# Mixing's output computed inside the scan's block, on the 32-column blocks of the diagonal

## The reference, cut to what matters

```python
def step(s, inp):
    q_, w_, k_, v_, a_, b_ = inp
    sa = jnp.einsum('bhij,bhj->bhi', s, a_)
    s = s * w_[:, :, None, :] + sa[..., None] * b_[:, :, None, :] + v_[..., None] * k_[:, :, None, :]
    return (s, jnp.einsum('bhij,bhj->bhi', s, q_))
...
mu = yg.mean(-1, keepdims=True)                       # over the 8 channels of a head
var = ((yg - mu) ** 2).mean(-1, keepdims=True)
y = ((yg - mu) / jnp.sqrt(var + EPS)).reshape(Bx, Tx, C) * ln_w + ln_b
rk = (r.reshape(Bx, Tx, H, HS) * k.reshape(Bx, Tx, H, HS) * time_faaaa.reshape(H, HS)).sum(-1, keepdims=True)
y = y + (rk * v.reshape(Bx, Tx, H, HS)).reshape(Bx, Tx, C)
return y * g @ Wo.T
...
x = _layernorm(x + mixing(x)); x = _layernorm(x + six_layers(x))
```

## Time and profile before

| what | us |
|---|---|
| median of 3 runs shown | 2058.27 (2057.75 to 2066.3) |
| the profiled execution's own time | 2050.26 |
| its span in the trace | 2048.5 |
| scan's last DVE instruction ends | 255.2 |
| first DVE instruction of the output's block | 260.86 |
| first product of the chain on PE | 283.11 |
| last start of the chain written by DVE | 321.87 |
| last part of the starts ends on PE | 336.9 |
| last copy of the output's block on ACT ends | 376.47 |
| first DVE instruction of the six layers' block | 379.30 |

### The profile page before, as it was taken

One profiled execution on the slowest core, in us unless ns is written; L12 is line 12 of the kernel. 1 busy time (PEld: TensorE's weight loads), 2 busy tenths in 40 slices (PEclk: granted clock), 3 DMA queues, 4 the chain that ended last, 5 costly groups with the idle time before them and its releaser, 6 DMA issues. The chain is left out here.

```text
span 2048.5 us, 74276 instructions
## 1 busy us (share of the span) xinstructions
PE 1858.8 (91%) x31234; PEld 1300.1 (63%) x31234; DVE 1515.7 (74%) x2858; ACT 1249.4 (61%) x2435; POOL 1225.9 (60%) x771
## 2 busy tenths in 40 slices
PE   7487778489999999999999999999999999999984
PEld 2254467156677776767666777677676767776762
DVE  6699854477778787777777787778777777878753
ACT  6422111366767767676767677676767676776761
POOL 3466610186767666766766676667666666766630
PEclk9799975699999999999999999999999999999996
DMA  4333000322222224232242222422324222222220
GB/s 98 53 40 43 1 21 0 142 68 64 71 62 70 65 64 121 63 75 63 71 116 69 63 68 65 118 66 64 74 64 122 64 68 63 68 65 63 70 59 21
DMA packets 89900, 137.41 MB, mean 67 GB/s; under 512 B 27296, under 2 KB 32864, under 8 KB 88544
## 3 DMA queue, kind: packets, MB, share of 16 engines
q1 hardware_dynamic: 89568, 132.67, 26.9%
HBM read 29.80 MB, written 2.10 MB: 16 GB/s over the span
## 5 line engine op out<-in xcount | busy, mean ns | idle before, releaser
L1086 POOL TENSOR_TENSOR qk<-qk,rnorm 128x1024 f32<-128x1024 f32 x192 | 361.1, 1902 | 369.6 <-ACT rnorm L1311 369.6
L1080 POOL TENSOR_TENSOR qk<-qk,turnedhalf 128x1024 f32<-128x1024 f32 x192 | 454.5, 2367 | 138.2 <-DVE turnedhalf L1437 138.2
L1433 DVE TENSOR_TENSOR qk<-bank,gains 128x512 f32<-128x512 f32 x384 | 262.1, 683 | 235.7 <-ACT squares L1301 224.5
L1137 PE MATMUL bank<-wqkv,x 128*128 128x512 f32 x768 | 378.6, 596 | 22.3 <-DMA qk_gain<-in_qk_gain 20.4
L1301 ACT ACTIVATE squares<-bank 128x512 f32<-128x512 f32 x384 | 232.8, 606 | 168.9 <-PE bank L1137 167.1
L1437 DVE TENSOR_TENSOR turnedhalf<-bank,gains 128x256 f32<-128x256 f32 x768 | 285.2, 412 | 0.0
L1348 ACT ACTIVATE o_T<-bank 128x512 f32<-128x512 f32 x192 | 104.2, 598 | 230.8 <-PE bank L1201 230.6
L1443 DVE TENSOR_REDUCE rnorm<-squares 128x16 f32<-128x1024 f32 x192 | 230.7, 1201 | 3.0 <-issue 0.2
L1201 PEld LDWEIGHTS bank<-p_T,v_win 64*64 64x64 f32 x12288 | 189.5, 135 | 59.4 <-issue 57.6
L1150 PEld LDWEIGHTS bank<-st_ident,qk 128*128 128x128 f32 x1536 | 178.0, 142 | 56.9 <-issue 50.7
L1201 PE MATMUL bank<-p_T,v_win 64*64 64x32 f32 x12288 | 201.3, 220 | 7.5 <-issue 7.4
(11 more groups left out here) (196 smaller groups left out, 3064.8 us busy)
## 6 DMA issues: line engine op xcount, KB each, us to landing
v_win<-v_tok SPq DMA_DIRECT2D x1536, 64.0 KB
wqkv<-in_wqkv SPq DMA_DIRECT2D x6, 1536.0 KB
v_rep_sb<-v_by_step SPq DMA_DIRECT2D x32, 128.0 KB
v_rep<-v_by_step SPq DMA_DIRECT2D x32, 128.0 KB
wo<-in_wo SPq DMA_DIRECT2D x6, 512.0 KB
w<-in_w SPq DMA_DIRECT2D x6, 341.0 KB
w<-in_w SPq DMA_DIRECT2D x6, 192.0 KB
xT_sb<-in_xT SPq DMA_DIRECT2D x1, 1024.0 KB, 4.7
```

The costliest lines, as they stand in the source:

```text
L1080: nc.gpsimd.tensor_tensor(out=qk[n % 2][:, half], in0=qk[n % 2][:, half], in1=turnedhalf[:, half], op=ALU.add).then_inc(rot_added.sem, 1)
L1086: nc.gpsimd.tensor_tensor(out=by_head(qk[u][:, half]), in0=by_head(qk[u][:, half]), in1=rnorm[u][:, AH * i:AH * (i + 1)].unsqueeze(2).to_b ...
L1137: nc.tensor.matmul(QK_BANKS[i][:, :], shifted_tokens(x, n, P), layer_cols(wqkv, n, 3 * INNER, 512 * i, 512), start=True, stop=True).then_i ...
L1433: nc.vector.tensor_tensor(by_head(qk[u][:, cols]), src, cos.to_broadcast([P, 8, DH]), ALU.mult).then_inc(rotated.sem, 1)
```

## The change

`build_scan` and `build_mix_output` become one function, `build_steps`, with one block. Its main parts:

- **End of the scan.** In the last step DVE makes the final G ahead of problem 0's last update: `end_g` into a PSUM bank, then spreads the first 8 chunks of each sequence (`spread_g_first`) and turns them with its own 32x32 transpose (`make_prop`). ACT copies G to SBUF (`copy_g`), POOL spreads the other 48 chunks (`spread_g`, 6 instructions), and DVE turns them at n = 4, 10 and 18 of the chain.
- **The diagonal.** A 128x128 block-diagonal matrix of 8x8 blocks has non-zeros only in four 32x32 blocks. `spread` and `prop` keep these alone: 32 columns for each chunk in place of 128. Each product of the chain and of `part_of_starts` is then four matmuls of 32 rows by 32 columns (`quads`), on the diagonal of the array.
- **Bonus.** rk on POOL in four pieces during the scan (`r_times_k`, at l = 2, 10, 18, 26), summed on PE at l = 25 to 28 (`product_rk`) with a matrix that has the vector in it, copied by ACT, multiplied with v by POOL during the chain.
- **During the chain.** The scan's last y product (8 matmuls, `last_y`) is issued two matmuls at a time behind chain(1) to chain(4). The parts of starts stand behind chain(9) to (12), (17) to (20), (25) to (28), (29) and (30), four products each; the last eight follow the chain. Groups 0 and 2 (the first half of each sequence) are centred, squared and scaled during the chain; `centre` is one matmul with (identity - ones/8) in place of a sum and a subtraction.
- **Behind the chain.** Groups 1 and 3 follow. For each group: `unit_y` (one operation, with ln_w in it), `gate_y` (two), the projection into one bank (4 matmuls), one addition of x for 512 columns, statistics, its own 1/sqrt as exp(-0.5 ln) on ACT, the norm, the turn, and two copies of 512 columns on ACT in place of eight of 128. The block's second ACT table load goes.

```diff
-def build_scan(nc, t, banks, v_dram, v_rep, state):
+def build_steps(nc, a, t, banks, v_dram, v_rep, state, y, zy, x_mid, x):
...
+            def make_prop(e, s):
+                cs = chunks(s, EIGHT * e, EIGHT * (e + 1))
+                if e:
+                    dve.wait_ge(g_spread.sem, B * (e - 1) + s + 1)
...
+                nc.vector.transpose(prop[:, cs, :].rearrange("p c m -> p (c m)"), spread[:, cs, :].rearrange("p c m -> p (c m)")).then_inc(prop_made.sem, 1)
...
             for l in range(CHUNK):
...
                 if l + 1 < CHUNK:
                     times_a(1, l + 1)
+                else:
+                    end_g()
+                    for s in range(B):
+                        spread_g_first(s)
+                    for s in range(B):
+                        make_prop(0, s)
                 renew0(l)
...
+            end_h()
...
+            for n in range(START):
+                next_start(n)
+                if n in (4, 10, 18):
+                    make_prop({4: 1, 10: 2, 18: 3}[n], 0)
+                    make_prop({4: 1, 10: 2, 18: 3}[n], 1)
+                if n == 20:
+                    whole_y(0)
+                if n == 21:
+                    whole_y(2)
+                if n == 27:
+                    unit_y(0)
+                if n == 28:
+                    unit_y(2)
+            whole_y(1)
+            whole_y(3)
+            gate_y(0)
+            gate_y(2)
+            add_x(0)
+            unit_y(1)
+            gate_y(1)
+            unit_y(3)
+            add_x(2)
+            gate_y(3)
+            norm_x(0)
+            add_x(1)
+            norm_x(2)
+            add_x(3)
+            norm_x(1)
+            norm_x(3)
...
+                if l % STEPS == 2:
+                    r_times_k(l // STEPS)
...
+            def quads(out, left, right, cols):
+
+                for q in range(P // QUAD):
+                    part = slice(QUAD * q, QUAD * (q + 1))
+                    mm = nc.tensor.matmul(out[part, cols], left[part], right[part], start=True, stop=True, skip_group_check=True)
+                return mm
...
+                    quads(CHAIN_BANKS[s], prop[:, c, :], start[:, c, :], slice(0, HS)).then_inc(chain_product.sem, 1)
...
+            for n in range(START):
+                chain(n)
+                if 1 <= n <= 4:
+                    last_y(2 * n - 2)
+                    last_y(2 * n - 1)
+                if 9 <= n <= 12:
+                    part_of_starts(2 * (n - 9), 2 * (n - 8))
...
+                if n == 22:
+                    centre(0)
+                if n == 23:
+                    centre(2)
+                if n == 24:
+                    variance(0)
+                if n == 25:
+                    variance(2)
...
+            part_of_starts(28, 32)
+            centre(1)
+            centre(3)
+            project(0)
+            variance(1)
+            project(2)
+            variance(3)
+            project(1)
+            turn_x(0)
+            project(3)
+            turn_x(2)
+            turn_x(1)
+            turn_x(3)
```

More of the change, by code:

```diff
@@ L459, in _ @@
                 in_step(l, stages)
+                if l == CHUNK - 1:
+                    copy_g()
                 copy_state(l)
@@ L575, in _ @@
                 in_step(l, stages)
-            dve.wait_ge(s_copied.sem, CHUNK)
-            last = decay[:, N:N + CHUNKS].unsqueeze(1).to_broadcast([P, HS, CHUNKS])
-            for p in range(2):
-                dve.wait_ge(s_new[p].sem, CHUNK)
-                nc.vector.tensor_tensor(rows(state[:, p, :]), rows(S_BANKS[p][:, :]), last, ALU.mult).then_inc(ended.sem, 1)
+            end_h()
+            for s in range(B):
+                nc.vector.memset(start[:, SEQ_CHUNKS * s, :], 0.0).then_inc(start_set.sem, 1)
@@ new lines, in _, with next_start @@
+            nc.vector.memset(x[64:P, :, 0:1], 0.0).then_inc(x_edged.sem, 1)
+            H = state[:, 0, :].rearrange("p (r c) -> p c r", c=CHUNKS)
+            def next_start(n):
+                for s in range(B):
+                    c = SEQ_CHUNKS * s + n
+                    dve.wait_ge(chain_product.sem, B * n + s + 1)
+                    if n == 0:
+                        dve.wait_ge(ended.sem, 1)
+                    nc.vector.tensor_tensor(start[:, c + 1, :], CHAIN_BANKS[s][:, 0:HS], H[:, c, :], ALU.add).then_inc(started.sem, 1)
@@ new lines, in norm_x @@
+            def norm_x(j):
+                dve.wait_ge(ln_made.sem, place(j) + 1)
+                for n in range(PER * j, PER * (j + 1)):
+                    nc.vector.tensor_scalar(x_mid[:, n, :], x_tok[:, n, :], ln_mv[:, n, 0:1], ln_mv[:, n, 1:2],
+                                            ALU.subtract, ALU.mult).then_inc(normed.sem, 1)
+            for n in range(START):
[11 more added lines that the diff above has]
+                    unit_y(2)
@@ new lines, in _, with last_y @@
+                if l >= CHUNK - STEPS + 1 and l < CHUNK - STEPS + 1 + GROUPS:
+                    product_rk(l - (CHUNK - STEPS + 1))
+            def last_y(i):
+                if i == 0:
+                    for p in range(2):
+                        pe.wait_ge(s_r[p].sem, CHUNK)
+                    pe.wait_ge(y_read.sem, y_read.after(CHUNK - 3))
+                mm = nc.tensor.matmul(Y_BANKS[(CHUNK - 1) % 2][:, 0:2 * CHUNKS], t["collect"][:, P * i:P * (i + 1)],
+                                      m2[:, (CHUNK - 1) % 2, i, :, :].rearrange("p s c -> p (s c)"), start=(i == 0), stop=(i == HS - 1))
+                if i == HS - 1:
+                    mm.then_inc(y_product.sem, 1)
@@ new lines, in centre, with variance @@
+            def centre(j):
+                pe.wait_ge(y_full.sem, place(j) + 1)
+                if place(j) == 0:
+                    pe.wait_ge(y_read.sem, y_read.after(CHUNK - 1))
+                if place(j) >= 2:
+                    pe.wait_ge(y_unit.sem, place(j) - 1)
+                nc.tensor.matmul(CENTRE_BANKS[place(j) % 2][:, :], head_centring[:, :], y[:, g_of[j]], start=True, stop=True).then_inc(centre_product.sem, 1)
+            def variance(j):
+                pe.wait_ge(y_squared.sem, place(j) + 1)
+                if place(j) >= 2:
+                    pe.wait_ge(y_log.sem, place(j) - 1)
+                nc.tensor.matmul(VAR_BANKS[place(j) % 2][:, :], t["headones"][:, :], ysq[:, g_of[j]], start=True, stop=True).then_inc(var_product.sem, 1)
@@ new lines, in project @@
+            def project(j):
+                pe.wait_ge(y_gated.sem, place(j) + 1)
+                if place(j) >= 2:
+                    pe.wait_ge(summed.sem, place(j) - 1)
+                else:
+                    pe.wait_ge(started.sem, B * START)
+                for i, n in enumerate(range(PER * j, PER * (j + 1))):
+                    mm = nc.tensor.matmul(O_BANKS[place(j) % 2][:, C * i:C * (i + 1)], yc[:, P * n:P * (n + 1)], t["w_o"][:, :], start=True, stop=True)
+                mm.then_inc(o_product.sem, 1)
```

432 lines of the change are left out of this document (231 added, 201 removed).

## The result

The changed kernel took 2001.01 us (median of 4, 1989.80 to 2003.68) where the kernel before took 2058.01 us on the same chip (median of 4, 2057.74 to 2066.30). The ratio is 0.9705, with a 95% interval of 0.9677 to 0.9732. The forecast was 2005 us, with a range of 1985 to 2030. The profiled execution took 1989.8 us with a span of 1988.0; for the same working the forecast was 1997.5.

What follows compares the result with a forecast made beforehand. PE was taken to bound the chain (126 products x 0.43 = 54 us), with DVE full before and behind it. Gains of 26.0 + 1.7 + 25.1 = 52.8 us from 2058.27 gave 2005 us, range 1985 to 2030.

Steps and rivals of the forecast that it cites:

- Start of the chain: From DVE's last `renew1` to PE's first chain product: first product at 257.1 in place of 283.1 us, a gain of 26.0.
- Rival D: In the scan: steps grow where rk's work stands, by up to 5 + 4 us, giving 2014 us; chance 0.07.
- One product of quads: On PE, four matmuls (eight records) take 0.20 us at half clock, between bounds of 0.10 and 0.43.
- Rival C: On PE: full clock kept, or tiles overlapping at half clock too; product 0.10 us, step 0.50, giving 1987 us; chance 0.15.
- B: On PE: quads overlap little, 0.40 us a product, 23 us more in all, giving 2028 us; chance 0.15.
- E: On PE: each small matmul costs 0.43 us, a product 1.71, about 186 us more, giving 2191 us; chance 0.03.
- The bare loop: In the chain: a step without other work takes 0.60 us, 31 steps 18.6 us.
- Last y product in pieces: In the chain: two matmuls behind each of four steps, records of 0.12 us, add 0.3 x 4 = 1.2 us.
- `centre` and `variance`: In the chain: four 128x512 matmuls in PE's queue, 1.69 us each at the lower clock, add 6.0 us.
- Waits for instructions: In the chain: stalls in PE's instruction stream, listed among the forecast's own bounds without a size.
- Behind the chain: From the last start to ACT's last copy: 29.5 us in place of 54.6, a gain of 25.1.
- The block's end: Between blocks: one block's end leaves the path; no change forecast from the last copy to the six layers' first transfer.

Runs made afterwards that it cites:

- the unused semaphores: The changed kernel with 40 more semaphores in its block that no engine uses; one run, 2000.29 us.
- early clears: The changed kernel with 50 of its block's 75 semaphores cleared by SyncE inside the block, 25 at its end; 1995.54 us, 0.9687 of the kernel before.

## Why the prediction was right, point by point

The median came 4 us below the forecast and inside the range. In the profile 7.7 us more went than the forecast's 52.8; 4.0 of these (the scan's end and the six layers) are scatter, which leaves 3.7 in the stretches that the change touches. That is partly luck: inside the chain an error of 7.6 us one way met 6.3 the other way, and the end of the block took 2.5 of the 5.8 that the chain and the tail gave beyond the forecast.

- **Start of the chain** (-26.0 forecast, -26.4). Right: transposes 0.38 for 0.41, spreads 0.38 for 0.41. (The forecast's "12 of 16 spreads" should be six of eight, by L717 x8; no term hangs on it.) That rk's fourth piece on POOL is covered held too: the scan doesn't end later. Rival D fell.
- **One product of quads** (0.20 forecast, 0.11 to 0.12). Mis-sized. The rows of the six layers gave 0.10 at full clock, and I doubled it for the clock at half. Both steps were too dear: on 32x32 tiles it is 0.07 to 0.09 at full clock (32 records in 0.27 us at 283.64 and in 0.36 at 284.63), and 0.11 at 0.50 granted, less than twice that. It was worth 14 x 0.54 = 7.6 us in the steps with parts, which grew by 0.06 in place of 0.6. Rival C had this half of the truth; B and E are ruled out by 14 to 15 ns a record. With them goes the rule of about 60 cycles a matmul (the Trainium skill, TensorEngine Tiling (Array Packing), Instruction Overhead), by which a record would take an estimated 50 ns at 1.2 GHz: the trace disagrees.
- **The bare loop** (0.60 a step, 0.58). Right; it is 0.53 where the clock is full.
- **Last y product in pieces** (+1.2 in all, about +2.9). Mis-sized: I took 0.12 us a record from full clock, and at half it was 0.29 (four in 1.15), steps up to 1.48. Whether it is better in pieces isn't shown.
- **`centre` and `variance`** (+6.0, and +6.0 by the four steps of 3.12, 2.29, 1.29 and 1.58 us). Right in sum by offsetting errors: `centre` took 2.0 for 1.69, with 0.9 of waiting ahead of the first, `variance` 1.1 at full clock for 1.69. The 1.69 was misread: from the row at 81.55 I took the lower level, but the granted clock rose to 1.00 ahead of its end (84.4), so it is a mixture of both.
- **Waits for instructions** (named as a risk, priced at nothing; 4.6 us). This is the term that was missing. It took back most of what the cheap product gave: -7.6 there, +4.6 here, +1.7 at the y product, and what remains, -2.1, in the loop, the transposes and small terms. Forecast 37.1, measured 33.73.
- **Behind the chain** (29.5 forecast, 27.04). The order and DVE's terms held. PE's granted clock was 1.00 from 298.1 to 304.9 us, and there a `project` took 1.05 in place of 2.0 (1.9 again behind it) and the last `variance` 1.0 in place of 1.69: `variance(3)` ended at 300.6, 11.8 us behind the chain and not 14.2.
- **The block's end** (nothing forecast, +2.5). Wrong. The gap of 5.64 us in the earlier trace rows was in plain sight, and I only counted that one such gap goes; I didn't ask what its length follows. It follows the number of semaphores: the 39 cleared at the end of the scan's block and the 32 at the end of the output's are 75 in one place now. The 2.2 us of clears that the first gap lost came back in the last one.

Of the forecast's conditions for being wrong, one came true in part: PE's granted clock was at 1.00 in the chain for 7 of its 33.7 us, from 281.0 to 287.9.

The chain is 33.7 us in the two profiles of the changed kernel, with a granted clock of 0.63 and 0.64, and 34.7 to 35.2 in four kernels whose clock is 0.59 to 0.61, although the clears and the unused semaphores touch nothing in it. The traces show why. In the changed kernel's profiles the clock rises at 281.0 and 281.8, ahead of both `variance`, which take 1.13 us each. In the four it rises at 285.5 to 286.9, and the two take 3.8 to 4.2 together, with early clears:

```profile
281.12 2.08 PE L1013 MATMUL bank<-w_sb,headones_sb 128*128 128x512 f32 x2
283.45 2.08 PE L1013 MATMUL bank<-w_sb,headones_sb 128*128 128x512 f32 x2
```

Their waits for issue are no longer in three of the four (4.2 to 4.6 us, against 4.6 and 5.0). So it is mainly the clock's level at two large matmuls, and differences of 1 to 2 us between chains can't be put down to an edit before that is looked at.

What stays open: why the clock rises later in kernels that don't differ ahead of that point, and why a packet of instructions starts only some time after PE has gone on with the one before. And the 26.4 us at the start of the chain and what the diagonal doesn't explain behind it (20 of 27.6 us) were read from the order and the durations of rows; no run took the joined blocks, the spreads or the shorter copies apart.

## What to carry to other kernels

A block-diagonal product belongs on the diagonal tiles of the array: four matmuls of 32x32 cost a quarter of one of 128 columns at the lower clock, but they are four times the instructions, and in a latency-bound chain the supply of these can be the next limit, so count PE's records against the time (here 128 in some 3.7 us). When an engine is freed, ask of each stretch which limit is second, for moving 6 us of work out of the chain returned only 3.6 there, and the stretch behind it took that back. And look at what stands between blocks: clearing semaphores is serial, here it is on the path, and it can be done earlier by an engine that idles.

## What the runs showed of the hardware

- Matmuls on four 32x32 tiles of the diagonal overlap: 14 to 15 ns from record to record at the lower clock (32 in 0.45 us), 8 to 11 at the full one (32 in 0.27 and in 0.36), where one record lasts about 0.2 us.
- PE waits for its own instructions, 0.2 to 1.9 us at a time, in places that lie multiples of about 128 records apart, where many short matmuls follow each other. Under load these places follow each other in 3.45 to 3.92 us, and packets of 16.4 KB in the queue "instruction" in step with them, one at a time, some 1.1 us each. The 4.6 us of such waits in the chain became 10.6 with 496 records more, and 0.5 with 224 fewer.
- Clearing a semaphore on SyncE takes 57 to 58 ns: 2.28 us for 40, 2.92 for 50; 39 clears follow each other in 2.2 us in the kernel before.
- DVE's own 32x32 transpose of a 128x256 fp32 tile takes 0.38 us, as an elementwise instruction of that shape does.
- A 128x512 matmul in fp32 took 2.0 us (its two records) at a granted clock of 0.50 and 1.0 to 1.2 at 1.00. The clock fell 2 us behind the first small matmuls (from 257.1) and rose behind two `centre` (281.0), or only behind both `variance` as well (285.5 in early clears).
